# Slot marks inverted in halves, two steps later, and the rotations of batch 1 spread out, in a fused attention and expert kernel

## The chip, the cores and the metric

One core of a Trainium2 chip runs the whole program. The metric is the device time of one execution in microseconds (us), as a median of several. Only the order of work inside the program differs between the kernel before and the changed one.

## What is computed

The input `x` holds 4 batches of 1024 rows of 128 numbers. It is normalised row by row to `xn`, and three terms are added:

```python
xn = _layernorm(x, axis=-1)
x = x + _L0_attn_ref(xn, W_q, W_k, W_v, W_o) + _L0_ffn_ref(xn, Wg, gamma, beta, W1, b1, W2, b2)
# attention: 16 heads of 8, rotary positions on Q and K, softmax over 1024 keys
Q = apply_rope(proj(W_q), pos, inv_freq);  K = apply_rope(proj(W_k), pos, inv_freq)
out = softmax(Q @ K.T / sqrt(8)) @ V ;  out @ W_o.T
# feed-forward: the best 2 of 8 experts for each row, weighted by a softmax of their two scores
w, idx = jax.lax.top_k(xf @ Wg, 2)
h = relu(normed @ W1[e] + b1[e]);  out = h @ W2[e] + b2[e] + xf ;  y = sum of w * out over the two experts
```

## The kernel before

Every engine has a program of its own, and they meet at semaphores. The attention sets the beat. It is cut into 256 **steps**, 64 for a batch and 16 for four heads. In step n TensorE (PE in the rows) first issues the scores of step n + 1, two units `u` of two matmuls each (line 494, tile `sc`), then `weigh(n)`, which multiplies the exponentials of step n with the values (line 527, tile `acc`), and then `aside(n)`, whatever else the tables of step numbers at the top of the file put into this step. ScalarE (ACT) makes the exponentials of every unit (line 710, tile `ring`), two a step. There are two score buffers, one for each unit: the scores of unit u of step n + 1 wait until ScalarE has read unit u of step n (`e_ok`). VectorE (DVE) goes through the same step numbers in `aside(n)`, but it is held only by the semaphores of what it reads and overwrites. Each eighth step begins with a `tail` on VectorE, which takes a finished `acc` tile (lines 854 to 861).

The asides around the change:

- **Marks.** Every row has two expert slots. VectorE's `mark(g)` (lines 980 to 985, four instructions) builds one of 8 groups of one-hot marks of these slots in steps 27, 29, ..., 41. TensorE's `invert(g)` (line 554, 8 matmuls for a group, all 64 accumulating in one tile of PSUM, `bank[1]`) turns them round into the list of the rows that belong to each slot, in steps 30, 32, ..., 44. There are two buffers of marks: `mark(g)` waits until `invert(g - 2)` is done (`mark_mm`).
- **Tokens.** `tokens()` on VectorE (lines 991 to 1008, step 46) makes row numbers of that list. GpSimd (POOL) then gathers rows for the first of 72 expert tiles (line 387, an indirect DMA for each tile).
- **Rotations.** `plain(b, r)` on TensorE (line 443, one 512-column matmul in float32, seen as two instructions) projects a quarter of the queries and keys of the next batch into `bank[0]`. VectorE rotates it in `take_plain` (lines 1015 and 1016) in the same step and in `split` (lines 1022 to 1029) in the next one. ScalarE squares the result (`SQUARE_AT`, line 716) between the exponentials of two steps; it waits for line 1023 there. For batch 1 the plains stand in steps 46, 48, 50 and 52.
- **Norms.** When the four squares of a batch are there, `head_norms(b)` on TensorE (line 457) and a maximum on VectorE (`bound`, line 777) follow in step `NORM_AT`, and `check_bound` and `decide` (lines 462 and 783 to 795) in step `FLAG_AT`. Both are computed from `SQUARE_AT`: the first step after the last square, two or more apart, in which an expert tile's second half and nothing of a first half stands, and which isn't a multiple of 8.
- **Expert tiles.** From step 54 on the steps alternate between the first half of a tile (`tile_in`, line 562, and `layer_one`, line 569, with `columns` and `relu` on VectorE, lines 1049 and 1056) and the second half (`layer_two`, line 577, with `rows_out` and `weights`, lines 1063 and 1043). `tile_in(0)` stands in step 53.

Of the kernel before, what the change touches and what calls it, by code (L numbers as in the profile page):

```python
# [41 lines left out]
GROUP = 8  # L42
GROUPS = 2 * T // GROUP
# [14 lines left out]
XH_AT = 18  # L58
ROUTE_AT, RANKS_AT, PLACE_AT, SLOTS_AT = 20, 21, 23, 24
MARK_AT = {27 + 2 * g: g for g in range(GROUPS)}  # L60
INVERT_AT = {30 + 2 * g: g for g in range(GROUPS)}
TOKENS_AT = 46
PLAIN_AT = {46 + 2 * r: (1, r) for r in range(4)}
PLAIN_AT.update({PER_BATCH * b + 37 + 4 * r: (b + 1, r) for b in range(1, B - 1) for r in range(4)})
SPLIT_AT = {n + 1: piece for n, piece in PLAIN_AT.items()}
SQUARE_AT = {n + 3: piece for n, piece in PLAIN_AT.items()}
PROJECT_AT = {PER_BATCH * (b + 1) + 3 + 2 * h: (b, h) for b in range(B - 1) for h in range(2)}
PROJECT_AT[STEPS - 4] = (B - 1, 0)

# [1 line left out]
FFN_FROM, DENSE_TILES = 54, 0  # L71
FREE_STEPS = [n for n in range(FFN_FROM, STEPS) if n not in PLAIN_AT and n not in PROJECT_AT]
FIRST, SECOND, WEIGHTS_AT = {}, {}, {}
used = 0
for t in range(SLOT_TILES):
# [10 lines left out]
LEAVES_BANK = [n for n in SECOND if n not in FIRST and n % KB]  # L86
NORM_AT = {min(n for n in LEAVES_BANK if n >= max(m for m in SQUARE_AT if SQUARE_AT[m][0] == b) + 1): b
           for b in range(1, B)}
# [6 lines left out]
def bank_uses():  # L95
# [3 lines left out]
    def take(k, *piece):  # L99
        count[k] += 1  # L100
        use[piece] = count[k]
# [5 lines left out]
    for n in range(STEPS):  # L107
# [8 lines left out]
        if n == RANKS_AT:  # L116
            take(1, "ranks")
        if n == min(INVERT_AT):
            take(1, "tokens")
        if n in PLAIN_AT:  # L120
            take(0, "plain", *PLAIN_AT[n])
        if n in NORM_AT:
# [20 lines left out]
def build(nc, x_d, wq_d, wk_d, wv_d, wo_d, wg_d, gamma_d, beta_d, w1_d, b1_d, w2_d, b2_d, cos_d, sin_d, const_d,  # L143
          out_d):
    ctx = ExitStack()
    with ctx:
# [3 lines left out]
        def sem(name):  # L150
            return ctx.enter_context(nc.semaphore(name))
# [95 lines left out]
        mark_ok, mark_mm, token_ok = sem("mark_ok"), sem("mark_mm"), sem("token_ok")  # L247
# [3 lines left out]
        bank_full = [sem(f"bank_full{k}") for k in range(2)]  # L251
# [151 lines left out]
        def _(pe):  # L403

            def enter_bank(k, *piece):
                wait(pe, bank_taken[k], USE[piece] - 1)
# [3 lines left out]
            for k in range(2):  # L410
                last = nc.tensor.transpose(acc[0][:, k * D:(k + 1) * D], wr[:, k, :], ident)
# [4 lines left out]
            def turn(b, h):  # L416
                if b == 0:
                    pe.wait_ge((xn_dve, xn_act)[h], 4)
                else:
                    pe.wait_ge(xn_pool, TB * (b - 1) + 4 * (h + 1))  # L420
                k = h if b == 0 else 0
                enter_bank(k, "turn", b, h)
                for u in range(4):
                    last = nc.tensor.transpose(bank[k][:, u * P:(u + 1) * P], xn[:, TB * b + 4 * h + u, :], ident)  # L424
                last.then_inc(bank_full[k], 1)
# [11 lines left out]
            def values(b, m):  # L437
                xnT_is_there(b, m // 2)
                enter_bank(1, "values", b, m)
                values_of(bank[1], b, m).then_inc(bank_full[1], 1)  # L440

            def project_qk(dst, b, c, k):
                return nc.tensor.matmul(dst, wT[:, k, :], xnT[:, b * S + c * CH:b * S + (c + 1) * CH], start=True,  # L443
                                        stop=True)

            def plain(b, r):
                c, s = ROPE_ORDER[r]
                enter_bank(0, "plain", b, r)
                project_qk(bank[0][:, :], b, c, 2 * s).then_inc(bank_full[0], 1)
# [10 lines left out]
            def check_bound(b):  # L460
                enter_bank(0, "bound", b)
                nc.tensor.transpose(bank[0][0:1, 0:P], norms[:, :], ident).then_inc(bank_full[0], 1)
# [4 lines left out]
            for r in range(4):  # L467
# [4 lines left out]
                for k in range(2):  # L472
                    last = project_qk(sc[r % 2][:, k * CH:(k + 1) * CH], 0, c, 2 * s + k)
# [58 lines left out]
            def turn_wo():  # L532
                pe.wait_ge(wo_sorted, 1)
                enter_bank(0, "wo")
                nc.tensor.transpose(bank[0][:, 0:D], wo_by_head[:, :], ident).then_inc(bank_full[0], 1)

            def turn_rows():
                pe.wait_ge(rows_in, 48)
                enter_bank(1, "rows")
                nc.tensor.transpose(bank[1][:, 0:48], rows[0:48, :], ident[0:48, 0:48]).then_inc(bank_full[1], 1)  # L540

            def ranks():
                pe.wait_ge(pick_ok, 1)
                enter_bank(1, "ranks")
                nc.tensor.matmul(bank[1][:, 0:T * E], before, cnt[:, 0, :, :], start=True, stop=True)
                nc.tensor.matmul(bank[1][:, T * E:2 * T * E], ones[:, :], cnt[:, 0, :, :], start=True, stop=True
                                 ).then_inc(bank_full[1], 1)

            def invert(g):
                pe.wait_ge(mark_ok, g + 1)  # L550
                if g == 0:
                    enter_bank(1, "tokens")
                for i in range(GROUP):
                    last = nc.tensor.matmul(bank[1][:, 0:2 * SLOT_TILES], place_mark[g % 2][:, i, :],  # L554
                                            named[g % 2][:, i, :, :].rearrange("p v c -> p (v c)"),
                                            start=(g == 0 and i == 0), stop=(g == GROUPS - 1 and i == GROUP - 1))
                last.then_inc(mark_mm if g < GROUPS - 1 else bank_full[1], 1)

            def tile_in(t):
                pe.wait_ge(xt_in[t % TILE_BUFFERS], 16 * (t // TILE_BUFFERS + 1))  # L560
                enter_bank(1, "tile", t)
                nc.tensor.transpose(bank[1][:, 0:P], xt[t % TILE_BUFFERS], ident).then_inc(bank_full[1], 1)  # L562

            def layer_one(t):
                pe.wait_ge(w_ok, t + 1)
                pe.wait_ge(bank_taken[1], USE["tile", t])
                enter_bank(0, "one", t)
                for c in range(FC):
                    last = nc.tensor.matmul(bank[0][:, c * P:(c + 1) * P], w_tile[t % 3][:, c * P:(c + 1) * P],  # L569
                                            xsT[t % 2], start=True, stop=True)  # L570
                last.then_inc(bank_full[0], 1)
# [10 lines left out]
            def project_out(b, h):  # L582
                pe.wait_ge(oT_ok, 2 * b + h + 1)
                enter_bank(0, "out", b, h)
                for i in range(4):
                    last = nc.tensor.matmul(bank[0][:, i * D:(i + 1) * D],  # L586
                                            oT[:, h * CH + i * P:h * CH + (i + 1) * P], woT[:, :], start=True,
                                            stop=True)
                last.then_inc(bank_full[0], 1)

            def aside(n):
                if n == WO_AT:
                    turn_wo()
                if n == COLUMNS_AT:
                    turn_rows()
                if n in TURN_AT:
                    turn(*TURN_AT[n])
                if n in VALUES_AT:
                    values(*VALUES_AT[n])
                if n == RANKS_AT:  # L600
                    ranks()
                if n in INVERT_AT:
                    invert(INVERT_AT[n])
                if n in PLAIN_AT:
                    plain(*PLAIN_AT[n])
                if n in PROJECT_AT:
                    project_out(*PROJECT_AT[n])
                if n == FFN_FROM - 1:
                    tile_in(0)
                if n in FIRST:  # L610
                    if FIRST[n] + 1 < SLOT_TILES:
                        tile_in(FIRST[n] + 1)
                    layer_one(FIRST[n])
                if n in SECOND:
                    layer_two(SECOND[n])
                if n in NORM_AT:
                    head_norms(NORM_AT[n])
                if n in FLAG_AT:
                    check_bound(FLAG_AT[n])
# [50 lines left out]
        def _(act):  # L670
# [36 lines left out]
            for n in range(STEPS):  # L707
                for u in range(2):
# [3 lines left out]
                                         ACT.Exp, scale=SCALE).then_inc(e_ok, 1)  # L712
                if n in SQUARE_AT:
                    b, r = SQUARE_AT[n]
                    act.wait_ge(sum_ok, 4 * (b - 1) + r + 1)
# [7 lines left out]
        def _(v):  # L723
# [356 lines left out]
            def aside(n):  # L1080
# [21 lines left out]
                if n in MARK_AT:  # L1102
                    mark(MARK_AT[n])
                if n == TOKENS_AT:
                    tokens()
# [90 lines left out]
```

## Time and profile before

| | |
|---|---|
| median of 3 runs | 671.93 us (671.84 to 672.0) |
| the profiled execution's own time | 671.26 us |
| its span, first to last instruction | 669.5 us |
| busy: PE, ACT, DVE, POOL | 621.7, 507.3, 387.9, 202.3 us |
| exponentials on ACT (line 710) | 512 of them, 491.9 us |

The profile shows one execution. A row of the timeline gives a start and a length in us, the engine (PEld is the weight load of TensorE), the line, the operation, output<-inputs, the shapes and how many instructions were merged into the row; in square brackets stands the idle time of the engine before it and what ended it. Matmuls of 512 columns overlap, so starts are a better guide than lengths. Below, the steps are named by the start of their `weigh`: step 32 is the one that starts at 109.25 us.

### The profile page before, as it was taken

How to read it: one execution, taken by the hardware profiler on the slowest of the kernel's cores; microseconds unless marked ns; L12 is line 12 of the kernel's file. 1: busy time of each engine (PE TensorE's matmuls, PEld its weight loads, DVE VectorE, ACT ScalarE, POOL GpSimd, SP SyncE). 2: the span in 40 equal slices, each digit the busy share in tenths (PEclk: the TensorE clock that was granted, in tenths of full speed). 3: DMA queues.
4: the chain of work that ended last, by engine and by line, in shares of the span. 5: the costliest groups of instructions: out<-in, count | busy, mean ns of one | idle time of the engine just before them, and what ended most of it. 6: DMA issues, size and time to landing. Idle time of an engine off the chain costs nothing.

```text
span 669.5 us, 12213 instructions
## 1 busy us (share of the span) xinstructions
PE 621.7 (93%) x4589; PEld 274.1 (41%) x4589; DVE 387.9 (58%) x1150; ACT 507.3 (76%) x551; POOL 202.3 (30%) x243
## 2 busy tenths in 40 slices
PE   3699998889999999999999999999999999999995
PEld 2224322222455555544455545544445455322222
DVE  3974669758655555587665555557766555344212
ACT  2387897888677777777777777778776777899992
POOL 0358200023763344323333343432344322100000
PEclk9889999999999999999999999999999999999997
DMA  6275702000230301200313031220031313461000
GB/s 225 55 203 155 189 1 64 0 17 21 71 88 24 87 25 48 72 17 20 83 28 86 25 87 29 52 64 17 21 87 35 73 21 76 162 198 49 16 0 34
DMA packets 25425, 43.99 MB, mean 66 GB/s; under 512 B 5472, under 2 KB 15248, under 8 KB 24848
## 3 DMA queue, kind: packets, MB, share of 16 engines
q1 hardware_dynamic: 20032, 32.15, 17.6%
q0 software_dynamic: 4608, 9.45, 5.2%
q10 hardware_dynamic: 720, 1.54, 0.6%
q8 instruction: 39, 0.64, 0.4%
q14 instruction: 26, 0.21, 0.1%
HBM read 17.43 MB, written 8.91 MB: 39 GB/s over the span
## 4 chain that ended last, share of the span: by engine, by line
PE 74%; ACT 11%; DVE 10%; issue 2%; DMA 1%; DVEq 1%; SPq 1%; POOL 0%; ACTq 0%
PE acc L527 28%; PE sc L494 16%; PE bank L577 12%; ACT ring L710 11%; PE bank L569 9%; PE bank L562 2%; PE bank L443 2%; PE bank L586 1%; DVE xn L1043 1%; PE bank L433 1%; PE bank L424 1%; DMA const<-shape_constants 1%; PE bank L554 1%; DVEq L1040 1%; SPq L292 1%
## 5 line engine op out<-in xcount | busy, mean ns | idle before, releaser
L710 ACT ACTIVATE ring<-sc 128x1024 f32<-128x1024 f32 x512 | 491.9, 1022 | 129.9 <-PE sc L494 129.1
L527 PE MATMUL acc<-ring,v 128*9 128x512 f32 x2048 | 270.0, 599 | 2.4 <-issue 2.4
L494 PE MATMUL sc<-qs,ks 32*128 32x512 f32 x1024 | 167.7, 500 | 19.2 <-ACT ring L710 13.0
L397 POOL DMA_INDIRECT token_out<-work,token x72 | 78.6, 1092 | 162.7 <-DVE work L1063 156.9
L387 POOL DMA_INDIRECT work<-normed,token x72 | 70.4, 978 | 172.2 <-DVE work L1049 103.0
L494 PEld LDWEIGHTS sc<-qs,ks 32*128 32x128 f32 x1024 | 65.0, 183 | 131.8 <-ACT ring L710 98.5
L577 PEld LDWEIGHTS bank<-xn,work 128*128 128x128 f32 x576 | 69.7, 191 | 65.6 <-DVE work L1056 37.7
L1056 DVE TENSOR_SCALAR work<-bank,xn 128x128 f32<-128x128 f32 x288 | 80.9, 343 | 25.3 <-PE bank L569 25.3
L577 PE MATMUL bank<-xn,work 128*128 128x128 f32 x576 | 83.1, 287 | 3.6 <-DVE work L1049 3.5
L569 PE MATMUL bank<-work,xn 128*128 128x128 f32 x576 | 77.0, 277 | 2.2 <-DVE norms L777 1.9
L569 PEld LDWEIGHTS bank<-work,xn 128*128 128x128 f32 x576 | 73.2, 197 | 4.1 <-DVE xn L1043 2.6
L1043 DVE COPY xn<-w_all 128x1158 f32 x72 | 55.6, 772 | 32.9 <-DVE work L1063 30.9
L1063 DVE TENSOR_TENSOR work<-bank,xn 128x128 f32<-128x128 f32 x72 | 20.9, 291 | 78.4 <-PE bank L577 78.2
L527 PEld LDWEIGHTS acc<-ring,v 128*9 128x9 f32 x2048 | 30.5, 88 | 66.4 <-issue 64.9
L854 DVE STREAM_TRANSPOSE blocks<-acc 128x512 f32<-128x512 f32 x32 | 22.7, 708 | 52.9 <-PE acc L527 52.8
L1049 DVE TENSOR_SCALAR work<-bank,xn 128x128 f32<-128x128 f32 x72 | 29.2, 406 | 11.4 <-PE bank L562 10.2
L562 PEld LDWEIGHTS bank<-const,work 128*128 128x128 f32 x72 | 10.0, 139 | 62.2 <-issue 62.2
L562 PE MATMUL bank<-const,work 128*128 128x128 f32 x72 | 23.6, 327 | 0.3
L377 POOL TENSOR_SCALAR xn<-xn,small 128x128 f32<-128x128 f32 x32 | 18.6, 596 | 5.6 <-DVE xnT L878 5.6
L392 POOL TENSOR_SCALAR x<-x,small 128x128 f32<-128x128 f32 x32 | 16.8, 534 | 0.3
L1036 DVE TENSOR_TENSOR x<-bank,x 128x512 f32<-128x512 f32 x8 | 5.5, 692 | 18.1 <-PE bank L586 18.1
L1015 DVE TENSOR_TENSOR turned<-bank,cos 128x512 f32<-128x512 f32 x12 | 8.3, 692 | 9.9 <-PE bank L443 9.9
(158 smaller groups left out, 312.2 us busy)
## 6 DMA issues: line engine op xcount, KB each, us to landing
qs<-hl SPq DMA_DIRECT2D x60, 128.0 KB
ks<-hl SPq DMA_DIRECT2D x60, 128.0 KB
w_all<-L_ffn_W SPq DMA_DIRECT2D x16, 256.0 KB, 4.9
x<-L_attn_x SPq DMA_DIRECT2D x4, 512.0 KB, 7.7
normed<-xn SPq DMA_DIRECT2D x4, 512.0 KB, 5.8
xn<-token_out SPq DMA_DIRECT2D x2, 1024.0 KB, 5.9
w_all<-token_out SPq DMA_DIRECT2D x2, 1024.0 KB, 10.4
out<-x SPq DMA_DIRECT2D x8, 256.0 KB, 2.2
```

Source lines behind the costliest of these rows:

```text
L387: pool.indirect_dma_start(out=xt[t % TILE_BUFFERS], out_offset=None, in_=xh_d[:, :], in_offset=bass.IndirectOffsetOnAxis(ap=token[:, 0, t: ...
L397: pool.indirect_dma_start(out=y_d[:, :], in_=ys[done % TILE_BUFFERS], in_offset=None, out_offset=bass.IndirectOffsetOnAxis(ap=token[:, 1, ...
L494: last = nc.tensor.matmul(dst, ks[r:r + 32, kb * P:(kb + 1) * P].bitcast(F32R), qs[r:r + 32, at].bitcast(F32R), start=True, stop=not slow)
L527: last = nc.tensor.matmul(acc[qh % 2][32 * j:32 * j + VW, :], v9[:, b, kb, 4 * g + j, :], ring[:, (2 * n + j // 2) % UNITS, j % 2, :], sta ...
L562: nc.tensor.transpose(bank[1][:, 0:P], xt[t % TILE_BUFFERS], ident).then_inc(bank_full[1], 1)
L569: last = nc.tensor.matmul(bank[0][:, c * P:(c + 1) * P], w_tile[t % 3][:, c * P:(c + 1) * P], xsT[t % 2], start=True, stop=True)
L577: last = nc.tensor.matmul(bank[1][:, 0:D], hT[t % 2][:, c, :], w_tile[t % 3][:, W2_AT + c * D:W2_AT + (c + 1) * D], start=(c == 0), stop=( ...
L710: nc.scalar.activation(ring[:, (2 * n + u) % UNITS, :, :], sc[u][:, :].rearrange("p (h c) -> p h c", h=2), ACT.Exp, scale=SCALE).then_inc( ...
L854: nc.vector.transpose(blocks[:, :, :].rearrange("p q r -> p (q r)"), acc[qh % 2][:, :]).then_inc(acc_out, 1)
L1043: nc.vector.tensor_copy(w_tile[t % 3], w_all[:, bass.ds(e, 1), :].rearrange("p o w -> p (o w)")).then_inc(w_ok, 1)
L1049: nc.vector.tensor_scalar(xsT[t % 2], bank[1][:, 0:P], w_tile[t % 3][:, GA_AT:GA_AT + 1], w_tile[t % 3][:, BE_AT:BE_AT + 1], ALU.mult, ALU.add
L1056: last = nc.vector.tensor_scalar(hT[t % 2][:, c, :], bank[0][:, c * P:(c + 1) * P], w_tile[t % 3][:, B1_AT + c:B1_AT + c + 1], 0.0, ALU.ad ...
```

## The change

`INVERT_AT` now holds two entries for a group: the first 4 matmuls of `invert(g)` stand in step 32 + 2g, the other 4 in step 33 + 2g. The wait for the marks stands before the first half, the signal after the second. So there are half inversions in every step from 32 to 47, where whole ones stood in 30, 32, ..., 44. `mark` stays where it was. `tokens` is in step 48 instead of 46. The plains of batch 1 stand in steps 43, 46, 49 and 52 instead of 46, 48, 50 and 52, and their splits one step behind each, as before. Every square stands four steps behind its plain instead of three, in all batches. From that the table of norms gives steps 119 and 183 for batches 2 and 3 instead of 117 and 181, and the flags steps 121 and 185 instead of 119 and 183; those of batch 1 stay in 57 and 59.

```diff
-INVERT_AT = {30 + 2 * g: g for g in range(GROUPS)}
-TOKENS_AT = 46
-PLAIN_AT = {46 + 2 * r: (1, r) for r in range(4)}
+INVERT_AT = {32 + 2 * g + part: (g, part) for g in range(GROUPS) for part in range(2)}
+TOKENS_AT = 48
+PLAIN_AT = {43 + 3 * r: (1, r) for r in range(4)}
...
-SQUARE_AT = {n + 3: piece for n, piece in PLAIN_AT.items()}
+SQUARE_AT = {n + 4: piece for n, piece in PLAIN_AT.items()}
...
-            def invert(g):
-                pe.wait_ge(mark_ok, g + 1)
-                if g == 0:
+            def invert(g, part):
+                if part == 0:
+                    pe.wait_ge(mark_ok, g + 1)
+                if (g, part) == (0, 0):
                     enter_bank(1, "tokens")
-                for i in range(GROUP):
+                for i in range(GROUP // 2 * part, GROUP // 2 * (part + 1)):
...
-                last.then_inc(mark_mm if g < GROUPS - 1 else bank_full[1], 1)
+                if part == 1:
+                    last.then_inc(mark_mm if g < GROUPS - 1 else bank_full[1], 1)
```

TensorE around steps 44 to 46, before: scores (`sc`), `weigh` (`acc`), the last whole inversion (`bank<-xn`) in step 44, nothing in 45, and the first plain (`bank<-xnT,wT`) in 46.

```order
L527 MATMUL acc<-ring,v 9x512 x4
L554 MATMUL bank<-xn 128x144 x8
L494 MATMUL sc<-qs,ks 128x512 x4
L527 MATMUL acc<-ring,v 9x512 x4
L494 MATMUL sc<-qs,ks 128x512 x4
L527 MATMUL acc<-ring,v 9x512 x4
L443 MATMUL bank<-xnT,wT 128x512
```

The same engine in steps 43 to 45 of the changed kernel, where line 554 has become 555 (behind the inversion its line numbers are two higher):

```order
L527 MATMUL acc<-ring,v 9x512 x4
L555 MATMUL bank<-xn 128x144 x4
L443 MATMUL bank<-xnT,wT 128x512
L494 MATMUL sc<-qs,ks 128x512 x4
L527 MATMUL acc<-ring,v 9x512 x4
L555 MATMUL bank<-xn 128x144 x4
L494 MATMUL sc<-qs,ks 128x512 x4
L527 MATMUL acc<-ring,v 9x512 x4
L555 MATMUL bank<-xn 128x144 x4
```

Every step has 4 matmuls of an inversion now, and step 43 has a plain behind them.

VectorE around the norm of batch 2, before: behind the weights' copy of step 117 (line 1043) the maximum (line 777), then the first half of a tile in step 118 (lines 1049 and 1056).

```order
L1043 COPY xn<-w_all 128x1158
L777 TENSOR_REDUCE norms<-bank 128x1
L1049 TENSOR_SCALAR work<-bank,xn 128x128
L1056 TENSOR_SCALAR work<-bank,xn 128x128 x4
L1063 TENSOR_TENSOR work<-bank,xn 128x128
```

In the changed kernel the same maximum (line 779) stands in step 119, and step 120 begins with a tail:

```order
L1045 COPY xn<-w_all 128x1158
L779 TENSOR_REDUCE norms<-bank 128x1
L856 STREAM_TRANSPOSE blocks<-acc 128x512
L859 RECIPROCAL rec<-blocks 128x16
L860 TENSOR_TENSOR att<-blocks,rec 128x16x8
L863 STREAM_TRANSPOSE oT<-att 128x512
L1051 TENSOR_SCALAR work<-bank,xn 128x128
L1058 TENSOR_SCALAR work<-bank,xn 128x128 x4
```

The tail lies between the maximum and the two operations for which TensorE's next steps wait; the flag's five small instructions, which stood right ahead of this tail, come two steps later.

## Rows read from the trace of the kernel before

**Rows 1.** The chain of work that ended last, by engine, from the page.

```profile
PE 74%; ACT 11%; DVE 10%; issue 2%; DMA 1%; DVEq 1%; SPq 1%; POOL 0%; ACTq 0%
```

**Rows 2.** Timeline from 574 to 590 us: steps with an empty aside.

```profile
578.93 3.77 ACT L710 ACTIVATE ring<-sc 128x1024 f32<-128x1024 f32 x4 [0.17 <-PE sc L494]
...
580.92 0.50 PE L494 MATMUL sc<-qs,ks 32*128 32x512 f32 x2 [0.21 <-ACT ring L710]
...
581.35 1.05 PE L527 MATMUL acc<-ring,v 128*9 128x512 f32 x8
...
582.32 0.93 PE L494 MATMUL sc<-qs,ks 32*128 32x512 f32 x4
...
582.87 3.77 ACT L710 ACTIVATE ring<-sc 128x1024 f32<-128x1024 f32 x4 [0.17 <-PE sc L494]
```

**Rows 3.** Timeline around the first inversion: steps 30 and 32.

```profile
102.88 1.05 PE L527 MATMUL acc<-ring,v 128*9 128x512 f32 x8
...
105.69 0.67 PE L554 MATMUL bank<-xn 128*128 128x144 bf16 x8 [1.75 <-DVE xn L985]
...
109.25 1.05 PE L527 MATMUL acc<-ring,v 128*9 128x512 f32 x8
```

**Rows 4.** Timeline of one later inversion, step 36; the x1 row is its last matmul.

```profile
115.92 3.77 ACT L710 ACTIVATE ring<-sc 128x1024 f32<-128x1024 f32 x4 [0.77 <-PE sc L494]
...
119.33 0.68 PE L554 MATMUL bank<-xn 128*128 128x144 bf16 x8
...
119.78 0.23 PE L554 MATMUL bank<-xn 128*128 128x144 bf16 x1
119.93 0.51 PE L494 MATMUL sc<-qs,ks 32*128 32x512 f32 x4
...
120.47 3.77 ACT L710 ACTIVATE ring<-sc 128x1024 f32<-128x1024 f32 x4 [0.77 <-PE sc L494]
```

**Rows 5.** Timeline: `weigh` of step 46 and of step 54, around the four plains.

```profile
141.07 1.05 PE L527 MATMUL acc<-ring,v 128*9 128x512 f32 x8
...
161.05 1.04 PE L527 MATMUL acc<-ring,v 128*9 128x512 f32 x8
```

**Rows 6.** Timeline and DMA issues: two marks, tokens, first gather, `tile_in(0)`, landing times.

```profile
112.97 1.22 DVE L980 TENSOR_TENSOR xn<-const,slot_hl 128x1024 bf16<-128x1024 f32 x1
...
116.04 1.23 DVE L980 TENSOR_TENSOR xn<-const,slot_hl 128x1024 bf16<-128x1024 f32 x1
...
138.21 0.31 DVE L991 COPY work<-bank 128x144 f32<-128x144 f32 x1 [6.07 <-PE bank L554]
...
141.38 1.19 POOL L387 DMA_INDIRECT work<-normed,token  x1 [66.49 <-DVE token L1008]
...
159.50 0.33 PE L562 MATMUL bank<-const,work 128*128 128x128 f32 x1
...
token_out<-work,token POOLq DMA_INDIRECT x72, 2.4
```

**Rows 7.** Timeline of ACT: the square in step 55, the exponentials after one in batch 2.

```profile
163.32 0.63 ACT L716 ACTIVATE xn<-turned 128x512 bf16<-128x512 f32 x1 [0.92 <-DVE turned L1023]
...
293.14 1.94 ACT L710 ACTIVATE ring<-sc 128x1024 f32<-128x1024 f32 x2 [0.77 <-PE sc L494]
```

**Rows 8.** Timeline of PE and DVE, steps 182 to 185, norm and flag of batch 3.

```profile
494.13 1.04 PE L527 MATMUL acc<-ring,v 128*9 128x512 f32 x8
...
495.15 0.68 DVE L777 TENSOR_REDUCE norms<-bank 128x1 f32<-128x512 f32 x1
...
495.98 1.13 PE L569 MATMUL bank<-work,xn 128*128 128x128 f32 x8 [0.54 <-DVE norms L777]
...
502.03 0.69 DVE L854 STREAM_TRANSPOSE blocks<-acc 128x512 f32<-128x512 f32 x1
...
504.29 1.12 DVE L1056 TENSOR_SCALAR work<-bank,xn 128x128 f32<-128x128 f32 x4
504.52 1.13 PE L577 MATMUL bank<-xn,work 128*128 128x128 f32 x8 [0.47 <-DVE work L1049]
```

More of the change, by code:

```diff
@@ L602, in aside @@
                 if n in INVERT_AT:
-                    invert(INVERT_AT[n])
+                    invert(*INVERT_AT[n])
                 if n in PLAIN_AT:
```

## Prediction

> **What bounds the kernel now.** I read the chain of work that ended last first: TensorE holds 74% of it, ScalarE 11%, VectorE 10% [rows 1]. So the price of an aside is what TensorE's part of the chain grows by, and where VectorE holds TensorE up, that wait is on it too. Then the timeline, in three places.
>
> *Steps with an empty aside.* The reader is to see one loop. ScalarE starts a unit at 578.93; two exponentials later TensorE may issue the scores of the second unit (580.92, 1.99 later), `weigh` follows 0.43 behind (581.35), the next scores 0.97 behind that (582.32), and ScalarE starts on them 0.55 later, at 582.87 [rows 2]. The loop takes 3.94 us and spans two steps, 1.97 a step. It holds one `weigh` and so one aside: **of two neighbouring steps the chain pays for one aside only**; the other runs while ScalarE has units in hand. A loop over three steps, which lets ScalarE go on for another step at 3.77 - 1.94 = 1.83 us [rows 2, 7], takes 3.94 + 1.83 = 5.77, which is 0.14 less than three steps at 1.97.
>
> *Inversions.* ScalarE's fresh starts are 4.55 apart (115.92 and 120.47) with 0.77 idle before each [rows 4]: 3.94 plus the 0.60 from the first matmul of the inversion (119.33) to the scores behind it (119.93). All eight stand in even steps, so the loop through the even steps pays for each in full, and the odd steps have nothing to hide. In the first one TensorE also waits for the marks [rows 3]: from `weigh` of step 30 (102.88) to that of step 32 (109.25) 6.37 us go by.
>
> *Plains.* Steps 46 to 54 take 161.05 - 141.07 = 19.98 us [rows 5], 5.00 for two, so a plain costs 5.00 - 3.94 = 1.06, and all four stand in even steps too.
>
> **The change, part by part.**
>
> 1. *The first wait.* The first half inversion stands two steps later. By then the marks have been ready for a while: they were at 105.69 [rows 3], and step 32's aside would begin at 102.88 + 3.94 + 0.97 = 107.8. Steps 30 and 31 are empty now and take 3.94 instead of 6.37: **-2.4 us**. Nothing else waited for the old moment: the marks of group 2 wait for the inversion of group 0, which I come to below.
>
> 2. *Halves in every step.* What half an inversion costs the trace doesn't show. Seven intervals between its matmuls take 119.78 - 119.33 = 0.45, 0.064 each, and from the last matmul to the scores 0.15 go by [rows 4], so 0.09 of the 0.60 belong to the passage and not to a matmul. Half is then 4 x 0.064 + 0.09 = 0.35, an estimate. From below it is 0.30 (half the whole), from above 0.60 (a passage as dear as the matmuls). I take 0.35, since the row resolves both parts. The Trainium skill, "TensorEngine Tiling (Array Packing)", Key Properties, says that changing the tiling mode drains TensorE, and an inversion (128 rows and columns) stands between `weigh` (9 columns a matmul) and scores (32 rows): it speaks against the change, which makes 16 such passages of 8. The trace agrees that there is a passage (0.15 against 0.064), and its size is in the sum; if the drain were larger than this row shows, the upper bound above is the case.
>  Now the steps from `weigh` of 32 to `weigh` of 54, 22 of them: 161.05 - 109.25 = 51.80 before [rows 3, 5], which is 11 x 3.94 + 7 x 0.60 + 4 x 1.06 = 51.8. After: 11 x 3.94 = 43.34; of sixteen halves the chain pays for those of one parity, 7 (odd steps 33 to 43, then 46) = 2.5; the plains in 43, 46, 49 and 52 change parity each time, so that it pays for all four, 4.24, but goes from one to the next by three loops of three steps, 3 x 0.14 = 0.4 less. That is 49.7. **-2.1 us**, of which 1.7 from the halves and 0.4 from the spacing.
>
> 3. *VectorE's side of it.* A mark takes 116.04 - 112.97 = 3.07 [rows 6]. `mark(g)` starts when the second half of g - 2 is done, in step 29 + 2g, and is wanted in step 32 + 2g. Three steps at (3.94 + 0.35) / 2 = 2.14 less the 0.35 give 6.1 us, against 3.07 and once, in step 40, a tail, of at most 2.3 (504.29 - 502.03 [rows 8], another operation included). The least slack is 0.7 us: **0**. If that cover were gone, TensorE would wait for what exceeds 6.1, and all behind it with it.
>
> 4. *Tokens.* The last half ends at about 142 instead of 138.1, and VectorE has more to do ahead of `tokens`. `weigh` of step 46 starts at 106.8 + 7 x 4.29 + 0.9 for the plain of step 43 = 137.7, that step's own half and plain end 2.4 later, at 140.1; then come six operations on 512 columns at 0.69 each, as line 854's [rows 8], and a tail of at most 2.3: `tokens` starts at 146.5 at the latest. With the 3.2 from the start of line 991 to the first gather (138.21, 141.38 [rows 6]) that gather is issued at 149.7. `tile_in(0)` wants it in step 53, at 155.0 (159.50 [rows 6] less parts 1 and 2). There were 18 us between the two, there will be 5.3. The landing of these gathers isn't shown; that of the scatters, of the same kind and size, is 2.4 us behind an issue of 1.2 [rows 6]: **0**, with 1.7 us to spare.
>
> 5. *Squares.* In the FFN steps of batch 2 ScalarE idles 0.77 behind each square's step [rows 7]; one step later a square of 0.63 falls into such a gap and delays nothing: 0. The square of step 55 makes ScalarE wait 0.92 for VectorE [rows 7]; it falls away, but TensorE had hardly anything to do in step 55: **-0.1**.
>
> 6. *Norms and flags of batches 2 and 3.* In step 182 the expert matmuls start 495.98 - 494.13 = 1.85 behind `weigh`, held up by the maximum [rows 8]; that wait moves to 184 and stays as dear. But there VectorE begins a tail behind the maximum. The maximum starts 1.02 behind `weigh` and takes 0.68; from the tail's start to the end of relu 504.29 + 1.12 - 502.03 = 3.38 go by [rows 8]; together that ends 5.1 behind `weigh`. TensorE wants relu 1.13 for its own matmuls [rows 8] and 0.43 + 0.97 [rows 2] behind 1.85, at 4.4. It will wait 0.7 where it waits 0.47 now [rows 8], 0.25 more. Twice: **+0.5**. Bounds: 0 (the flag's 1 us ahead of the tail is saved as well) and 2 x 0.7.
>
> Sum: -2.4 - 2.1 - 0.1 + 0.5 = -4.1. Against its own span that makes 669.5 into 665.4. The profiled execution took 671.26, 0.7 less than the median of the runs, 671.93; taking the same 4.1 from the median gives **667.8**.
>
> **The rivals.**
>
> - *Half an inversion costs nearly a whole one* (0.60 instead of 0.35). For: each needs its own passage between the shapes. Against: the 0.45 and 0.15 above. Part 2 would lose 7 x 0.25 = 1.75: **669.5**.
> - *VectorE's marks become the beat.* Before, `mark(g)` had four steps between two inversions, now three. It would take 0.7 us more than I count in the group with the tail, or 3 in each of the others. A partial wait of 1 to 3 us: **669 to 671**.
> - *The first gather isn't there in time.* TensorE would stand in step 53 at `tile_in(0)`, with scores, `weigh` and all later steps behind it. It is hidden if the gather lands within 5.3 us of its start; the kernel is slower than before if it takes more than 5.3 + 4.1 = 9.4. Against it stands the 2.4 us of the scatters; for it, that the trace has no landing of a gather. At 12 us: 667.8 + 12 - 5.3 = **674.5**. This is the case on the other side.
> - *More is hidden than I count*: halves at 0.30, the norms' tail free: **667.0**.
> - *Nothing comes of it*, since what is gained up to step 54 is given back behind it, in a wait for some transfer or event at a fixed time: **671.9**. I find none in the chain: behind step 54 it is matmuls and the VectorE work of the same steps.
>
> **How the numbers follow.** Forecast (667.2 to 668.6) 0.72; halves nearly whole (to 669.5) 0.11; marks or a late gather that cost 1 to 3 us 0.06; more hidden (under 667.2) 0.06; nothing 0.02; slower 0.03. The range from 667.0 to 669.5 holds the forecast, the first rival and most of the last but one. A difference of 0.2%, 1.3 us, is about what a measurement of this kernel can tell from none. Faster by more than that, below 670.6: 0.91; within 0.05; slower 0.04.
>
> **What would show it right or wrong.** In the profile after, the first half inversion shows no idle time that line 987 ends; `weigh` of step 32 starts at 106.9 and that of step 54 at about 156.7; two steps with halves take 4.3 us, and the stretch from the first of four matmuls to the scores 0.35. ScalarE's idle of 0.77 in every second step is gone for shorter ones. TensorE's wait at line 579 behind the flag of batches 2 and 3 grows to 0.7. The prediction would be wrong if a wait for line 987 or for a gather appears, if halves come out at over 0.45, or if steps from 54 on take longer than before.

## The result and the profile after

The changed kernel takes 665.02 us (median of 4, 664.81 to 665.9) against 671.96 (4 runs), a ratio of 0.9907 with an interval of [0.9892, 0.9921]. It is faster, as forecast, but by 6.9 us where 4.1 were forecast, and lies 2 us below the stated range. Two further groups of runs gave 665.28 against 671.53 and 665.19 against 671.70, so 6.2 to 6.9. The profiled execution took 665.9 with a span of 664.1; it is the slowest of its four, so the account below is made from differences between steps and not from the span.

The chain of work that ended last answers to [rows 1]: TensorE has gained share, VectorE has lost it.

```profile
PE 78%; ACT 10%; DVE 7%; issue 2%; DMA 1%; DVEq 1%; SPq 1%; POOL 0%; ACTq 0%
```

The timeline of steps 32 to 34 answers to [rows 3] and [rows 4]. The inversions (line 555) come as 4 and 4.

```profile
103.15 1.05 PE L527 MATMUL acc<-ring,v 128*9 128x512 f32 x8
...
107.09 1.05 PE L527 MATMUL acc<-ring,v 128*9 128x512 f32 x8
...
108.07 0.42 PE L555 MATMUL bank<-xn 128*128 128x144 bf16 x4
...
109.20 1.05 PE L527 MATMUL acc<-ring,v 128*9 128x512 f32 x8
110.17 0.42 PE L555 MATMUL bank<-xn 128*128 128x144 bf16 x4
110.53 0.92 PE L494 MATMUL sc<-qs,ks 32*128 32x512 f32 x4
...
111.38 1.05 PE L527 MATMUL acc<-ring,v 128*9 128x512 f32 x8
```

Steps 30 and 31 take 107.09 - 103.15 = 3.94 us, where 6.37 went by before, and no idle time stands before line 555. The marks of the eight groups are ready 2.16 to 3.55 us ahead of their first half inversion. Half an inversion costs 110.53 - 110.17 = 0.36 up to the scores, and the two steps from 107.09 to 111.38 take 4.29.

In step 43 a half inversion and a plain stand together:

```profile
131.65 0.42 PE L555 MATMUL bank<-xn 128*128 128x144 bf16 x4
131.91 1.07 PE L443 MATMUL bank<-xnT,wT 128*128 128x512 f32 x2
132.91 0.51 PE L494 MATMUL sc<-qs,ks 32*128 32x512 f32 x4
```

The two take 132.91 - 131.65 = 1.26 us up to the scores, where their separate prices, 0.35 and 1.06, add up to 1.41.

The rows that answer to [rows 6] are those of the first gather and of `tile_in(0)`:

```profile
148.50 1.19 POOL L387 DMA_INDIRECT work<-normed,token  x1 [73.35 <-DVE token L1010]
...
155.01 0.33 PE L564 MATMUL bank<-const,work 128*128 128x128 f32 x1
```

TensorE takes the tile 6.5 us behind the issue of its gather, and its row shows no wait.

Those that answer to [rows 8], the norm of batch 3 in its new place, steps 184 and 185:

```profile
494.12 1.05 PE L527 MATMUL acc<-ring,v 128*9 128x512 f32 x8
494.22 0.76 DVE L1045 COPY xn<-w_all 128x1158 f32 x1 [0.47 <-DVE work L1065]
494.90 0.68 DVE L779 TENSOR_REDUCE norms<-bank 128x1 f32<-128x512 f32 x1
495.50 0.70 DVE L856 STREAM_TRANSPOSE blocks<-acc 128x512 f32<-128x512 f32 x1
495.73 1.13 PE L571 MATMUL bank<-work,xn 128*128 128x128 f32 x8 [0.31 <-DVE norms L779]
...
497.49 0.37 DVE L1051 TENSOR_SCALAR work<-bank,xn 128x128 f32<-128x128 f32 x1
497.78 1.12 DVE L1058 TENSOR_SCALAR work<-bank,xn 128x128 f32<-128x128 f32 x4
498.21 1.16 PE L579 MATMUL bank<-xn,work 128*128 128x128 f32 x8
```

Here is what the forecast didn't have. TensorE starts line 579 at 498.21, with no wait, while line 1058 (relu) still runs until 498.90. It doesn't want this relu: the tables of steps give `layer_two` in step 185 the tile before the one that line 1058 works on, and that tile's relu was done two steps earlier. What it wants is `bank[1]` back from the columns, line 1051, and these ended at 497.86.

With the starts of `weigh` in the two traces the time can be put into places, in us:

| from `weigh` of step to that of step | before | after | forecast of the difference |
|---|---|---|---|
| 28 to 32 | 10.31 | 7.88 | -2.4 |
| 32 to 54 | 51.80 | 49.47 | -2.1 |
| 54 to 57 | 7.77 | 7.66 | -0.1 |
| 117 to 124 | 20.16 | 19.08 | +0.25 |
| 181 to 188 | 19.81 | 19.07 | +0.25 |

The differences are -2.43, -2.33, -0.11, -1.08 and -0.74, together -6.7, near the 6.2 to 6.9 of the medians. The table isn't the whole account: the steps left out from 57 on (57 to 117, 124 to 181, 188 to the end) take 1.1 more in this trace of the changed kernel than in the one before. They differ by 0.7 between traces of the changed kernel too, so these two traces can't tell whether any of the 1.1 belongs to the change.

### The profile page after: what moved, and what is told of

Same layout as the page of the kernel before. It is cut to its first block, busy times and chain, and to the rows that moved or that the text cites. A ratio compares the mean times of both kernels' runs of the same rounds, so it can differ in the third digit from the quotient of the medians.

```text
span 664.1 us, 12213 instructions
## 1 busy us (share of the span) xinstructions
PE 624.2 (94%) x4589; PEld 275.0 (41%) x4589; DVE 388.1 (58%) x1150; ACT 508.1 (77%) x551; POOL 202.5 (30%) x243
## 4 chain that ended last, share of the span: by engine, by line
PE 78%; ACT 10%; DVE 7%; issue 2%; DMA 1%; DVEq 1%; SPq 1%; POOL 0%; ACTq 0%
PE acc L527 30%; PE sc L494 18%; PE bank L579 12%; ACT ring L712 10%; PE bank L571 9%; PE bank L564 2%; PE bank L443 2%; PE bank L588 1%; DVE xn L1045 1%; PE bank L433 1%; PE bank L424 1%; DMA const<-shape_constants 1%; PE bank L555 1%; SPq L292 1%; DVEq L1042 1%
## 5 line engine op out<-in xcount | busy, mean ns | idle before, releaser
L494 PE MATMUL sc<-qs,ks 32*128 32x512 f32 x1024 | 169.6, 500 | 14.2 <-ACT ring L712 9.2
L370 POOL TENSOR_SCALAR xn<-x,small 128x128 f32<-128x128 f32 x24 | 10.5, 451 | 10.5 <-DVE small L768 10.5
```

Source lines behind the costliest of these rows:

```text
L494: last = nc.tensor.matmul(dst, ks[r:r + 32, kb * P:(kb + 1) * P].bitcast(F32R), qs[r:r + 32, at].bitcast(F32R), start=True, stop=not slow)
```

## The experiments

Each is timed against the kernel before on the same chip. There are three groups, each on a chip of its own, and the one with the whole groups, the earlier halves and both experiments on the plains holds no changed kernel; its medians are set against the 665.02 to 665.28 of the others. In three traces of the changed kernel the stretches from 28 to 57, 117 to 124 and 181 to 188 repeat to a few hundredths of a us, which the whole time doesn't; so each experiment is read from them first. Step 58 doesn't repeat so well: 3.28, 3.16 and 3.14.

### The changed kernel again

> The changed kernel again, as the measure for the others of this group. Theory A (the place of the norms of batches 2 and 3 gives about 1.8 us, everything up to step 54 gives 4.7): about 6.5 us below the kernel before, weigh of step 54 some 4.5 to 4.8 earlier than before and step 200 some 6. If the first measurement was partly luck, nearer to 5.5.

> The changed kernel once more, as the measure for this group: weigh of step 54 57.35 us behind that of step 28, steps 117 to 124 in 19.1 us.

Nothing is edited. 665.28 us (ratio 0.9904 [0.9886, 0.9921]) and 665.19 (0.9901 [0.9885, 0.9916]). `weigh` of step 54 stands 57.35 and 57.34 behind that of step 28, steps 117 to 124 take 19.09 and 19.06, steps 181 to 188 take 19.07 in both. The result holds.

### Which part gives the gain behind step 54

```diff
-SQUARE_AT = {n + 4: piece for n, piece in PLAIN_AT.items()}
+SQUARE_AT = {n + 3: piece for n, piece in PLAIN_AT.items()}
```

> The changed kernel with every square three steps behind its plain again, so that the norms stand in 117 and 181 and the flags in 119 and 183 as before. Theory A: steps 117 to 124 and 181 to 188 lose what they gained, about 1.0 and 0.7 us, so 1.8 us slower than the changed kernel; up to step 54 within 0.2 us of it. Rival (the steps from 54 on gained by something earlier, such as other timing of the gathers): as fast as the changed kernel. My forecast on record, that the norms' new place costs 0.5 us, would make this one 0.5 us faster.

666.88 us (0.9934 [0.992, 0.9948]), 1.6 slower than the changed kernel in the same group. Steps 181 to 188 take 19.80 again, steps 117 to 124 take 19.90. The forecast on record had this one faster; it is refuted. But steps 28 to 54 take 57.72 here, 0.37 more than in the changed kernel, where I expected at most 0.2: in step 46 ScalarE waits 0.66 for VectorE ahead of its square. So with the plains of batch 1 three steps apart their later squares are worth something as well, and this run doesn't isolate the norms. The next two do.

The norms' place alone, in the kernel before:

```diff
+NORM_AT = {57: 1, 119: 2, 183: 3}
```

> The kernel before with only the norms of batches 2 and 3 moved to steps 119 and 183 and the flags to 121 and 185; squares, marks, plains as before. Theory A: 1.8 us faster than before, the wait of line 577 behind the flag (0.48 and 0.47 us, ended by line 1049) gone, the wait for the maximum 0.2 to 0.3 shorter. Theory B (the later squares make the gain): no difference.

670.19 us (0.9976 [0.9966, 0.9986]), 1.3 less than before. Steps 117 to 124 take 19.08, 181 to 188 take 19.08, as in the changed kernel; that is 1.8 less, as expected, and the interval, 0.9 to 2.3 us, holds both.

The squares of batches 2 and 3 one step later, in the kernel before, with the norms that follow:

```diff
-SQUARE_AT = {n + 3: piece for n, piece in PLAIN_AT.items()}
+SQUARE_AT = {n + 3 + (piece[0] > 1): piece for n, piece in PLAIN_AT.items()}
```

> The kernel before with the squares of batches 2 and 3 one step later, from which the norms' new places follow; batch 1 as before. Theory A: the same as with the norms alone, 1.8 us faster than before, since each square lies in idle time of the scalar engine in either place. Theory B: more than with the norms alone, by the waits of 0.5 us that four squares have now.

669.92 us (0.9977 [0.9968, 0.9986]): the same as with the norms alone, and 19.08 in both stretches. So theory A stands: the later squares themselves give nothing that could be measured in these batches. The norm and the flag that they push along give everything.

What of it is the flag's, what the norm's? The flag alone, in the kernel before:

```diff
-FLAG_AT = {min(m for m in LEAVES_BANK if m >= n + 2): b for n, b in NORM_AT.items()}
+FLAG_AT = {59: 1, 121: 2, 185: 3}
```

> The kernel before with only the flags of batches 2 and 3 in steps 121 and 185; the norms stay in 117 and 181. Theory A' (the wait of line 577 in steps 121 and 185 is for the columns of line 1049, which stand behind flag and tail; with the flag's five small instructions gone from there it vanishes): 0.5 us a batch, steps 181 to 188 in 19.3 instead of 19.8 us, and the wait for the maximum in step 182 unchanged; with the norms moved too it was 19.1. Rival (the flag's instructions only lie in idle time, the norm's place makes all the gain): 19.8.

670.91 us (0.9991 [0.998, 1.0003]), by the whole time not to be told from before. The steps tell it: 181 to 188 take 19.36, 0.45 less than before, and 117 to 124 take 19.31. Its timeline of steps 182 to 185:

```profile
493.66 0.77 DVE L1043 COPY xn<-w_all 128x1158 f32 x1 [0.73 <-DVE work L1063]
494.34 0.69 DVE L777 TENSOR_REDUCE norms<-bank 128x1 f32<-128x512 f32 x1
...
495.17 1.13 PE L569 MATMUL bank<-work,xn 128*128 128x128 f32 x8 [0.56 <-DVE norms L777]
...
502.27 0.37 DVE L1049 TENSOR_SCALAR work<-bank,xn 128x128 f32<-128x128 f32 x1
502.55 1.12 DVE L1056 TENSOR_SCALAR work<-bank,xn 128x128 f32<-128x128 f32 x4
502.79 1.13 PE L577 MATMUL bank<-xn,work 128*128 128x128 f32 x8
```

The wait of 0.47 before line 577 [rows 8] is gone, since the columns (line 1049) now end at 502.64, ahead of it. Before, five small instructions of the flag stood on VectorE ahead of the tail, and the columns behind both. The wait for the maximum is still 0.56. The remaining 0.28 come with the norm: in its new place that wait is 0.31, since the copy ahead of the maximum comes sooner (a gap of 0.47 before it instead of 0.73).

In that gap lies the read of the expert's number (line 1040 or 1042) with which the weights' copy begins. In all three traces with the norms in 117 and 181 (the kernel before, the squares back, the flag alone) the reads of the copies beside these two maxima take 522 to 912 ns; in the other eleven, with the norms in 119 and 183, they take 299 to 314. Batch 2 shows what that costs TensorE: with reads of 912, 637 and 522 ns, step 118 takes 3.70, 3.43 and 3.31, which differ by as much as the reads. In the kernel before TensorE waits twice as long there as in batch 3:

```profile
329.61 1.13 PE L569 MATMUL bank<-work,xn 128*128 128x128 f32 x8 [0.90 <-DVE norms L777]
```

So 0.39 of the 0.85 that the flag alone seems to give from step 117 to 124 is a shorter read in step 118; the flag itself is worth 0.45 in either batch. And what the norm's new place gives, 0.6 in batch 2 and 0.2 to 0.3 in batch 3, follows the read: step 120 takes 0.60 less than step 118 did with a read 0.61 shorter, step 184 takes 0.23 less than step 182 with a read 0.24 shorter.

### Why the marks are cheaper

The groups whole again, at the new place:

```diff
-INVERT_AT = {32 + 2 * g + part: (g, part) for g in range(GROUPS) for part in range(2)}
+INVERT_AT = {32 + 2 * g: g for g in range(GROUPS)}
...
-                    invert(*INVERT_AT[n])
+                    invert(INVERT_AT[n], 0)
+                    invert(INVERT_AT[n], 1)
```

> The changed kernel with each group's 8 matmuls together again, in steps 32, 34, ..., 46; all else as changed. Theory A (of two neighbouring steps the chain pays one aside, so what an inversion costs is the larger of the two sums): two steps take 4.55 again instead of 4.30 and the first wait stays gone, weigh of step 54 some 1.3 us later than in the changed kernel, the whole 1.2 to 1.5 us slower than it. Rival (the halves are as dear together as the whole, and the gain is from the later start and the spacing): no difference from the changed kernel.

666.52 us (0.9928 [0.9914, 0.9942]), 1.2 to 1.5 more than the changed kernel. Steps 28 to 32 take 7.87, so the first wait stays gone; steps 32 to 54 take 50.92 instead of 49.47, 1.45 more. The splitting alone is worth that, and the rival falls.

The groups cut into 6 and 2:

```diff
-                for i in range(GROUP // 2 * part, GROUP // 2 * (part + 1)):
+                for i in (range(6), range(6, GROUP))[part]:
```

> The changed kernel with the groups cut into 6 and 2 matmuls instead of 4 and 4; the same matmuls, the same steps. Theory A (the chain pays only the larger of two neighbouring asides): two steps take 3.94 + 0.48 = 4.42 instead of 4.30, so weigh of step 43 stands 0.6 us later than in the changed kernel and that of step 54 0.5 us. Rival (only the sum counts): no difference.

665.9 us (0.9916 [0.9902, 0.9929]). TensorE's timeline shows the pattern, with the passage behind the larger part and a wait for ScalarE behind the smaller one:

```profile
115.42 1.05 PE L527 MATMUL acc<-ring,v 128*9 128x512 f32 x8
116.40 0.55 PE L555 MATMUL bank<-xn 128*128 128x144 bf16 x6
...
117.31 1.05 PE L527 MATMUL acc<-ring,v 128*9 128x512 f32 x8
118.29 0.30 PE L555 MATMUL bank<-xn 128*128 128x144 bf16 x2
...
119.41 0.50 PE L494 MATMUL sc<-qs,ks 32*128 32x512 f32 x2 [0.39 <-ACT ring L712]
119.84 1.05 PE L527 MATMUL acc<-ring,v 128*9 128x512 f32 x8
```

Two steps take 119.84 - 115.42 = 4.42, as expected, against 4.29 or 4.30. From step 32 to 42, five pairs, it is 22.10 against 21.48, the 0.6 expected. Up to step 43 it is only 0.42, since step 42 is one of the short ones, and up to 54 it is 0.48 against the 0.5 expected. The same matmuls in the same steps cost more when they are uneven: the chain pays the larger of two neighbouring asides.

The splitting without the later start:

```diff
-INVERT_AT = {32 + 2 * g + part: (g, part) for g in range(GROUPS) for part in range(2)}
-TOKENS_AT = 48
+INVERT_AT = {30 + 2 * g + part: (g, part) for g in range(GROUPS) for part in range(2)}
+TOKENS_AT = 46
```

> The changed kernel with the halves two steps earlier, in steps 30 to 45, and tokens in 46: the splitting without the later start. Theory A: the wait for the marks of group 0 comes back with 1.8 us, about as the trace before shows it, and weigh of step 54 stands 1.6 us later than in the changed kernel. Rival (a later start only moves the wait to later groups): no difference. The marks of each group have the same three steps here.

666.64 us (0.9918 [0.9903, 0.9934]), 1.4 to 1.6 more than the changed kernel in the other groups. The wait is back at its old place and with its old size:

```profile
105.95 0.42 PE L555 MATMUL bank<-xn 128*128 128x144 bf16 x4 [1.76 <-DVE xn L987]
```

Up to step 54 it is 59.08 from step 28 against 57.35, 1.73 more (expected 1.6). The later start doesn't move the wait to later groups.

### The plains

Back in steps 46, 48, 50 and 52:

```diff
-PLAIN_AT = {43 + 3 * r: (1, r) for r in range(4)}
+PLAIN_AT = {46 + 2 * r: (1, r) for r in range(4)}
...
-SQUARE_AT = {n + 4: piece for n, piece in PLAIN_AT.items()}
+SQUARE_AT = {n + 3 + (piece[0] > 1): piece for n, piece in PLAIN_AT.items()}
```

> The changed kernel with the plains of batch 1 in steps 46, 48, 50 and 52 and their squares three steps behind; halves, tokens and batches 2 and 3 as changed. Theory A: the last half and the first plain fall together in step 46, each plain costs 1.06 instead of 0.92 and the square of step 51 waits for the vector engine by about 1.2 us, since a tail and the tokens stand ahead of its rotation; weigh of step 54 about 1.1 us later than in the changed kernel. Rival (only the marks matter): no difference.

666.12 us (0.9921 [0.9908, 0.9935]). Steps 43 to 54 take 27.02 instead of 25.89, 1.13 more, as expected, with the wait that was expected on ScalarE:

```profile
149.18 0.63 ACT L718 ACTIVATE wr<-turned 128x512 bf16<-128x512 f32 x1 [1.05 <-DVE turned L1025]
```

So the new place of plains and squares together is worth more in the changed kernel than the 0.4 that I gave the spacing. Step 51, where this wait stands, takes 2.88 instead of 2.53: 0.35 of the 1.13 come from the rotation, which stands behind a tail and the tokens on VectorE. The other 0.8 lie in the rest of these steps; no run takes spacing and squares apart there.

Each plain in two halves of 256 columns:

```diff
+HALF_PLAIN_AT = {n - 1 + half: (b, r, half) for n, (b, r) in PLAIN_AT.items() if b == 1 for half in range(2)}
...
+            def half_plain(b, r, half):
+                c, s = ROPE_ORDER[r]
+                if half == 0:
+                    enter_bank(0, "plain", b, r)
+                at = b * S + c * CH + half * (CH // 2)
+                last = nc.tensor.matmul(bank[0][:, half * (CH // 2):(half + 1) * (CH // 2)], wT[:, 2 * s, :],
+                                        xnT[:, at:at + CH // 2], start=True, stop=True)
+                if half == 1:
+                    last.then_inc(bank_full[0], 1)
...
-                if n in PLAIN_AT:
+                if n in HALF_PLAIN_AT:
+                    half_plain(*HALF_PLAIN_AT[n])
+                elif n in PLAIN_AT:
```

> The changed kernel with each plain of batch 1 in two halves of 256 columns as well, in steps 42 and 43, 45 and 46, 48 and 49, 51 and 52; the rotations stay where they are. A half costs about 0.43 plus a passage of 0.2, so 0.63. Theory A with its one-step loop (scores to weigh 0.43, weigh 0.97, plus the aside, against 1.97 for an empty step): 1.40 + 0.63 is 2.03 already, so both halves are on the chain and nothing is gained, weigh of step 54 within 0.3 us of the changed kernel or a little later. Rival (what is halved is half hidden, whatever its size): 4 x (1.06 - 0.63), less the 0.4 of the spacing, 1.3 us faster than the changed kernel.

665.25 us (0.9904 [0.9888, 0.9919]), and `weigh` of step 54 is 57.32 behind that of step 28, against 57.35: nothing is gained. Its timeline of TensorE, steps 48 to 50 (lines 457 and 538 are the half plain and `weigh` here):

```profile
142.51 1.05 PE L538 MATMUL acc<-ring,v 128*9 128x512 f32 x8
143.49 0.70 PE L457 MATMUL bank<-xnT,wT 128*128 128x256 f32 x2
144.12 0.50 PE L505 MATMUL sc<-qs,ks 32*128 32x512 f32 x4
144.56 1.05 PE L538 MATMUL acc<-ring,v 128*9 128x512 f32 x8
145.53 0.70 PE L457 MATMUL bank<-xnT,wT 128*128 128x256 f32 x2
146.16 0.99 PE L505 MATMUL sc<-qs,ks 32*128 32x512 f32 x4
```

A half costs 144.12 - 143.49 = 0.63, and step 48 takes 144.56 - 142.51 = 2.05, bound by TensorE alone as expected: 1.40 us (scores and `weigh`) and the half together are more than the 1.97 of an empty step. With half an inversion the sum is 1.76, and it fits. But this isn't the whole reason. Step 49 takes 2.52 and step 50 2.35, and in both TensorE waits for ScalarE. There a square (146.49, 0.63 long) stands ahead of the exponentials that start at 147.00; by the 0.55 from scores to exponentials [rows 2] they could have started at about 146.7, an estimate. The three steps take 6.9 us, as in the changed kernel (6.83); both halves in full would make 5.77 + 2 x 0.63 = 7.03, one alone 6.40. So that nothing is gained is shown; how much of it is the second half's and how much the square's is not.

### A faster version

The wait for the maximum that is left (0.31 in the rows above, 0.48 in step 58 of the same trace) is for a maximum that stands behind the weights' copy. In the changed kernel it is put ahead of it:

```diff
                 if n in SECOND:
                     rows_out(SECOND[n])
+                if n in NORM_AT:
+                    bound(NORM_AT[n])
                 if n in WEIGHTS_AT:
                     weights(WEIGHTS_AT[n])
...
-                if n in NORM_AT:
-                    bound(NORM_AT[n])
```

> The changed kernel with the vector engine's maximum of the norms ahead of the weights' copy of the same step instead of behind it, in batches 1, 2 and 3. If the wait of the expert matmuls for the maximum is that copy's 0.7 us, it goes: step 58 takes 0.5 to 0.7 less than its 3.28, steps 120 and 184 some 0.5 less than their 3.11, together 1.6 us faster than the changed kernel. If the weights are then late for the next tile, less. No difference would mean that the maximum waits for something else.

663.52 us (0.9877 [0.9858, 0.9896]) against 665.19 of the changed kernel in the same group, 1.7 less. Step 58 takes 2.57 instead of 3.14 to 3.28, steps 120 and 184 take 2.56 instead of 3.10 and 3.11. Steps 183 to 185 in its timeline:

```profile
492.31 0.69 DVE L779 TENSOR_REDUCE norms<-bank 128x1 f32<-128x512 f32 x1
492.62 1.05 PE L527 MATMUL acc<-ring,v 128*9 128x512 f32 x8
493.06 0.77 DVE L1045 COPY xn<-w_all 128x1158 f32 x1
...
493.76 1.06 PE L571 MATMUL bank<-work,xn 128*128 128x128 f32 x8
```

The expert matmuls start 1.14 behind `weigh`, where they started 495.73 - 494.12 = 1.61 in the changed kernel. The copy starts 0.44 behind `weigh` instead of 0.10, and costs its readers nothing more: TensorE waits for this copy at three tiles, 0.8 us together, in both kernels. Steps 121 and 185 take 0.07 longer. The order also takes the maximum out of the reach of a slow read.

## Why the prediction was right in its direction and wrong in its size

1. *The first wait*, -2.4: -2.43, right, and shown by undoing it alone: the wait is back with 1.76 us, steps 28 to 32 take 10.06, and 1.73 is left of it at step 54, since the halves also end two steps sooner there.
2. *Halves in every step*, -2.1: -2.33, right, with a half at 0.35 to 0.36 for the forecast 0.35. The rule that of two neighbouring steps the chain pays one aside is shown by the uneven cut and by the whole groups. That a half could cost nearly a whole one is refuted. The loop over three steps is there too: from `weigh` of step 49 to that of 52 it takes 6.82, where 5.77 + 1.06 were forecast. The sum had each half and each plain at its full price in steps 43 and 46; there the two together take 1.26 instead of 1.41, which is worth 0.3 and more than covers the 0.2 between forecast and measurement. How the 2.1 were divided, 1.7 for the halves and 0.4 for the spacing, no run confirms: undone one at a time they cost 1.45 and 1.13, squares included, more than 2.33 together.
3. *VectorE's side*, 0: right, no inversion waits for marks from step 32 on. The least slack is 2.2 us, in the first group, for the 0.7 of the forecast, which was a bound.
4. *Tokens*, 0: right; the first gather was issued 6.5 us ahead of its reader, for the 5.3 that I bounded. When it lands no row shows.
5. *Squares*, -0.1: -0.11, and none in batches 2 and 3, right. That with the new spacing the later squares of batch 1 save another 0.37 up to step 54 wasn't in the reasoning; the sum didn't need it, since it took the spacing without such a wait.
6. ***Norms and flags*, +0.5: this step failed.** It measured -1.08 and -0.74, together -1.8, so 2.3 of the 2.6 us between the forecast sum and the measured one. The prediction has TensorE want relu "at 4.4" and goes on: "It will wait 0.7 where it waits 0.47 now". TensorE's wait there is for the columns, and the row had said so: it names line 1049, not 1056 [rows 8]. I had paired `layer_two` with the relu of the step ahead, where the table of steps gives it the tile before. The tail's length up to the columns stands in the trace before:

```profile
504.01 0.37 DVE L1049 TENSOR_SCALAR work<-bank,xn 128x128 f32<-128x128 f32 x1
```

With the right reader the same sum reads: 1.02 for the start of the maximum, 0.68, the tail's 504.01 - 502.03 = 1.98 and 0.37 for the columns make 4.05 behind `weigh`, under the 4.4 at which TensorE comes. So the wait of 0.47 goes and nothing takes its place. I had named the flag's 1 us ahead of the tail, but only as a way to a bound of 0. To let that bound stop at no change was the second mistake: the wait was in the trace, its cause was moved away, and the range had to take in that it goes, 2 x 0.5.

The third lies in the sentence ahead of these, that the wait for the maximum "stays as dear" in its new place. It fell from 0.54 to 0.31 in batch 3 and from 0.90 to 0.30 in batch 2; with the flag's part that makes 0.74 and 1.08. This the rows of batch 3 alone couldn't have told: it hangs on how long a read takes, 554 and 912 ns in the trace before and 313 and 304 in the trace after. How much of it a single trace of the kernel before shows is luck in part: its 912 is the longest of the six such reads in three traces.

The rivals of a slower or an equal time had no part in it.

## What to carry to other kernels

In a loop of two engines with two buffers between them, work put aside between the loop's instructions is paid by the larger of two neighbouring steps: cut it evenly over both. Here that paid where each part and the engine's own work fitted into an empty step (1.76 of 1.97 us), and not in the one try where they didn't (2.03). Read the releaser's line in a wait's row, and find in the table of steps which tile each reader belongs to, before costing what a later producer does. A small reduction that frees a buffer for the bound engine belongs ahead of a long copy that nobody waits for yet.

## What the hardware showed that I had not expected

VectorE's weights copy begins with a read of the expert's number from on-chip memory into a register (line 1040). It takes 304 ns as a median and up to 912:

```profile
L1040 DVEq TENSOR_LOAD <-owner x72: 299/304/912, 158.3 to 561.9; - x72
```

Most of the slow ones fall into loads of the query and key copies (line 292), whose issues go on for some 5 us. In the kernel before, at the norm of batch 2:

```profile
322.62 2.40 SPq L292 DMA_DIRECT2D qs<-hl  x4
...
328.10 0.77 DVE L1043 COPY xn<-w_all 128x1158 f32 x1 [1.07 <-issue]
```

The gap before the copy is 0.46 in most steps and 1.07, 0.71, 0.50 or 0.77 about 5.1 to 5.6 us behind the start of such a load (at 322.62, 489.36, 390.67 and 516.39), though not behind every one, and once 0.83 without one. In steps 117 and 181 the maximum stood right behind this copy, and the delay went to TensorE; two steps later the read was short in every trace, and the slow one had fallen where nobody waits. That slow reads and loads coincide is all that the traces show; what makes the read slow wasn't tried.
